# Graph transformer layer on one core: the front in seven parts, GpSimd making the centred rows of eight of 25 blocks

## The chip, the cores and the metric

One core of a Trainium2 chip runs the whole program. The metric is the device time of one execution in microseconds (us). Before the change it is 783.42 us, the median of three runs (782.71 to 783.50).

## What is computed

The input x has 6250 rows of 256 values. A layer norm gives `xn`. Three branches are added to x: a graph attention (four heads), a mixing branch of 1x1 convolutions in hyperbolic space, and, behind a second layer norm, a routed feed-forward layer. The change concerns only how the first two branches begin:

```python
xn = _layernorm(x, axis=-1)
# graph branch
xt = jnp.matmul(x, weight).reshape(-1, heads, out_ch)
alpha_l = jnp.einsum('ehd,hd->eh', xt[row], attn_l)
alpha_r = jnp.einsum('ehd,hd->eh', xt[col], attn_r)
# mixing branch
h = logmap0(proj(x, c), c)
h = conv1d(jnp.transpose(h, (1, 2, 0)), w_qkv, pad=2)   # one row long: a 256 x 768 product
```

`proj` clips the norm of a row and `logmap0` scales the row by arctanh(norm)/norm, so both branches need, for each row of x, its mean, its variance and a factor from the norm.

## The kernel before

The rows are cut into 25 blocks of 250 rows (125 partitions, two rows t to a partition). The program has one written-out order of instructions for each engine; engines meet at semaphores only. The **front** is all that stands before the first product with `w_qkv` (L1242). For a block b it does this:

- SyncE (SP) loads x in twelve loads (`LOADS`, L75, issued at L524): eight at the start, four later, each behind the store of a block named in `LOAD_AFTER` (L428).
- VectorE (DVE), `row_sums(b)` (L1627): two bn_stats. Then, for a **part** of several blocks at once (`PARTS`, L76: 2, 3, 4, 5, 6 and 5 blocks), the factors of its rows are worked out on tiny tiles (125 x 4 to 125 x 12): `row_square` (nine instructions, L1638 to L1652), two powers on GpSimd (POOL, L612 and L613), `row_clip` (three, L1658 to L1662), two logarithms on ScalarE (ACT, `row_logs`, L851 and L852), and `row_factors` (five, L1668 to L1676).
- DVE, `make_h(b)` (L1687): two tensor_scalar of 125 x 256, (x - mean) * factor, into a ring `hb` of four blocks (`HS`). It waits for the turn of block b-4.
- TensorE (PE), `turn_h(b)` (L1187): four transposes into PSUM bank b % 2. ACT, `keep_h(b)` (L893): one copy of 128 x 500 to SBUF.
- PE, `make_xt(b)` (L1199): four products of that copy with the graph weights, 125 x 264 each half. It waits for `keep_h(b)` and for `keep_xt(b - 2)`, which frees its bank. ACT, `keep_xt(b)` (L901): two copies with a scale. SP (L549) stores these rows to `xt_table` in HBM, from where GpSimd later gathers them (L623, L626).

The order around the change is written out by hand. PE turns block b and then makes the table rows of block b-1; ACT follows in the same order, with the parts' logarithms and the later weight loads (`later_load`, L861 to L887) between. `idle_work` (L1165) is a number of products whose result nobody reads; they stand where PE would otherwise wait. Before all this PE turns the graph weights (L1171) once they have landed (`wg_in`), ACT copies them (L847), PE multiplies them with the attention vectors (L1177) and ACT copies the result beside the weights (L857, `prep`), for which `make_xt(0)` waits. In the program before, `row_logs(0)` stands behind the copy of L847.

Behind the front PE runs the 75 steps of the QKV product (L1242), which start when the table rows of block 23 are kept, then the rest.

## Time and profile before

| | |
|---|---|
| median of three runs | 783.42 us (782.71 to 783.50) |
| profiled execution, device time | 782.98 us |
| its span, from the first to the last instruction | 780.8 us |
| PE busy | 746.4 us, 96% of the span |
| DVE, ACT, POOL busy | 587.1, 497.2, 510.4 us |
| first QKV product (L1242) | 74.25 us from the span's start |

Times in the trace are microseconds from the start of the span. The record of an instruction lasts until its result is written, and the next one on the same engine may start before that. So the spacing of starts tells what an instruction occupies, its end what a waiting engine sees. A PE product or transpose in f32 leaves one or two records: 36 records are 18 idle products, 8 are the four products of one `make_xt`, 4 the transposes of one `turn_h`.

### The profile page before, as it was taken

How to read it: one execution, taken by the hardware profiler on the slowest of the kernel's cores; microseconds unless marked ns; L12 is line 12 of the kernel's file. 1: busy time of each engine (PE TensorE's matmuls, PEld its weight loads, DVE VectorE, ACT ScalarE, POOL GpSimd, SP SyncE). 2: the span in 40 equal slices, each digit the busy share in tenths (PEclk: the TensorE clock that was granted, in tenths of full speed). 3: DMA queues.
4: the chain of work that ended last, by engine and by line, in shares of the span. 5: the costliest groups of instructions: out<-in, count | busy, mean ns of one | idle time of the engine just before them, and what ended most of it. 6: DMA issues, size and time to landing. Idle time of an engine off the chain costs nothing. (4 is left out here: it accounts for less than half of the span.)

```text
span 780.8 us, 17022 instructions
## 1 busy us (share of the span) xinstructions
PE 746.4 (96%) x5582; PEld 629.9 (81%) x5582; DVE 587.1 (75%) x1726; ACT 497.2 (64%) x1153; POOL 510.4 (65%) x693
## 2 busy tenths in 40 slices
PE   7999999999899999999929989999999999999996
PEld 7888888888666666666626678999999999999996
DVE  7973488788769988888897865666777667767676
ACT  2565335989899888888828616555555555555550
POOL 3340778777458888888826652676677766867654
PEclk9999999999999999999968999999999999999999
DMA  8665122222102211111110113000000000000001
GB/s 232 201 176 158 42 58 50 61 47 58 30 20 70 61 51 44 52 35 60 28 43 26 37 33 103 6 23 27 14 27 20 22 28 16 26 27 15 27 21 46
DMA packets 35546, 41.43 MB, mean 53 GB/s; under 512 B 11636, under 2 KB 20812, under 8 KB 35455
## 3 DMA queue, kind: packets, MB, share of 16 engines
q1 hardware_dynamic: 22471, 30.71, 13.1%
q0 software_dynamic: 8000, 6.82, 4.0%
q10 hardware_dynamic: 4984, 2.79, 1.5%
q8 instruction: 45, 0.74, 0.4%
q14 instruction: 46, 0.38, 0.2%
HBM read 25.59 MB, written 14.60 MB: 51 GB/s over the span
## 5 line engine op out<-in xcount | busy, mean ns | idle before, releaser
L1242 PE MATMUL ps<-Z,L 128*128 128x250 f32 x600 | 126.9, 373 | 0.0
L1242 PEld LDWEIGHTS ps<-Z,L 128*128 128x128 f32 x600 | 113.6, 189 | 13.2
L1097 ACT ACTIVATE Z<-Z,b1s 128x250 f32<-128x250 f32 x144 | 70.0, 503 | 70.5 <-DVE Z L2212 70.5
L1362 PE MATMUL ps<-wr,Z 128*125 128x256 f32 x400 | 92.7, 384 | 0.0
L942 ACT ACTIVATE Z<-Z,bn_o,bn_s 128x250 f32<-128x250 f32 x150 | 81.2, 599 | 1.0 <-DVE bn_o L1920 1.0
L1362 PEld LDWEIGHTS ps<-wr,Z 128*125 128x125 f32 x400 | 73.1, 188 | 10.2 <-issue 0.4
L1104 ACT ACTIVATE L<-ps 128x250 f32<-128x250 f32 x144 | 54.3, 379 | 42.1 <-PE ps L1492 40.1
L2212 DVE TENSOR_TENSOR Z<-ps,L 128x250 f32<-128x250 f32 x144 | 59.7, 416 | 18.3 <-PE ps L1492 15.9
L1252 PE MATMUL ps<-Z,pw 64*64 64x250 f32 x600 | 54.6, 386 | 15.6 <-issue 14.9
L1801 DVE BATCH_NORM_STATS2 L<-Z 128x6 f32<-128x250 f32 x140 | 49.3, 408 | 25.9 <-ACT Z L938 22.3
L623 POOL DMA_INDIRECT L<-xt_table,idst x36 | 44.2, 1228 | 34.8 <-issue 33.7
L938 ACT ACTIVATE Z<-ps 128x500 f32<-128x500 f32 x75 | 43.4, 579 | 30.9 <-PE ps L1242 24.5
L776 POOL TENSOR_TENSOR L<-Z 128x500 f32<-128x500 f32 x23 | 31.8, 1381 | 44.8 <-ACT Z L1097 44.8
L1492 PE MATMUL ps<-Z 128*128 128x250 f32 x192 | 56.4, 375 | 0.2 <-ACT Z L1097 0.2
L626 POOL DMA_INDIRECT asrc<-xt_table,isrc x40 | 48.4, 1210 | 12.2 <-issue 12.2
L1252 PEld LDWEIGHTS ps<-Z,pw 64*64 64x64 f32 x600 | 25.7, 133 | 36.5 <-issue 26.3
L1340 PE MATMUL ps<-L,ones 128*32 128x250 f32 x600 | 48.5, 384 | 2.0 <-ACT L L970 1.0
L1199 PE MATMUL ps<-L,Z 128*125 128x264 f32 x200 | 48.8, 388 | 0.8 <-ACT Z L893 0.5
L1531 PEld LDWEIGHTS ps<-Z 128*125 128x125 f32 x368 | 47.2, 187 | 2.0
L1531 PEld LDWEIGHTS ps<-L 128*125 128x125 f32 x368 | 47.1, 187 | 2.0
L1531 PE MATMUL ps<-Z 128*125 128x128 f32 x368 | 47.6, 272 | 0.0
L1531 PE MATMUL ps<-L 128*125 128x128 f32 x368 | 47.5, 272 | 0.0
(280 smaller groups left out, 2006.2 us busy)
## 6 DMA issues: line engine op xcount, KB each, us to landing
Z<-in_x SPq DMA_DIRECT2D x25, 250.0 KB
out<-L SPq DMA_DIRECT2D x24, 250.0 KB
xt_table<-L SPq DMA_DIRECT2D x25, 231.0 KB
Z<-in_x SPq DMA_DIRECT2D x4, 672.0 KB
Z<-in_x SPq DMA_DIRECT2D x5, 448.0 KB
g_table<-gg SPq DMA_DIRECT2D x25, 62.5 KB
gg<-g_table SPq DMA_DIRECT2D x25, 62.5 KB
Z<-in_w SPq DMA_DIRECT2D x2, 512.0 KB, 3.7
```

The lines of the kernel that those rows point to most:

```text
L942: a_.activation(zc(b, c), zc(b, c), ACT.Relu, bias=bn_o[:, c:c + 1], scale=bn_s[:, c:c + 1]).then_inc(done.sem, 1)
L1097: a_.activation(to, of, ACT.Gelu, bias=b1s[:, f // NF, f % NF:f % NF + 1]).then_inc(gelu_done, 1)
L1104: a_.activation(kp[:, s, k - 1], ps[:, bank, 0:BT], ACT.Copy).then_inc(product_kept[s].sem, 1)
L1199: last = mm(ps[0:TP, 2 + 2 * (b % 2) + t, 0:XT], h_raw(b, k)[:, t * TP:(t + 1) * TP], wg[:, k, :], start=(k == 0), stop=(k == KD - 1))
L1242: last = mm(ps[:, group_bank(n), h * BT:(h + 1) * BT], wq[:, k, c * 128:(c + 1) * 128], h_raw(b, k), start=(k == 0), stop=(k == KD - 1))
L1252: return mm(to[cols_], lhsT[rows_, HALF * a:HALF * a + HALF], rhs[rows_], start=True, stop=True)
L1340: last = mm(ps[32 * q:32 * q + 32, 5, 0:BT], ones[:, 0:32], of, start=(i == 0), stop=(i == 3), skip_group_check=True)
L1362: last = mm(res_bank(b, t), ob(b, c, 1)[:, t * TP:(t + 1) * TP], wr[:, c, :], start=(c == 0), stop=(c == NO - 1))
L1492: mm(ps[:, bank, 0:BT], of, by, start=first, stop=True, skip_group_check=True).then_inc(product[s].sem, 1)
L1531: last = mm(ps[0:TP, bank, 0:HD2], of[:, k], by[:, k], start=(first and k == 0), stop=(k == NF - 1), skip_group_check=True)
L1801: v_.bn_stats(to, ps[:, group_bank(n), h * BT:(h + 1) * BT] if last else zc(b, c)).then_inc(z_sums.sem, 1)
L2212: v_.tensor_tensor(to, ps[:, bank, 0:BT], kp[:, s, k - 1], ALU.add).then_inc(product_sum[s].sem, 1)
```

## The change

- `PARTS` has seven parts, of 1, 2, 3, 4, 5, 5 and 5 blocks.
- GpSimd makes the centred rows of blocks 0, 1, 2, 4, 6, 8, 11 and 12 (`POOL_H`) with the same tensor_scalar as DVE, written between the powers of the parts; DVE makes the other 17.
- PE turns block b and then makes the table rows of block b-2 in place of b-1, in the steady part; near the start some go in pairs. Idle products go from 18, 2, 3, 3 and 10 to 12, 2, 10, 2 and 4.
- ACT: `row_logs(0)` stands ahead of the copy of the turned graph weights, and all `row_logs` have new places.
- DVE has a new order of sums, parts and rows.
- The load of blocks 16 and 17 goes out behind the store of block 1 in place of block 0.

```diff
-    PARTS = ((0, 2), (2, 5), (5, 9), (9, 14), (14, 20), (20, NB))
+    PARTS = ((0, 1), (1, 3), (3, 6), (6, 10), (10, 15), (15, 20), (20, NB))
+    POOL_H = (0, 1, 2, 4, 6, 8, 11, 12)
...
-        FIRST_LOADS, LOAD_AFTER = 8, (0, 2, 3, 5)
+        FIRST_LOADS, LOAD_AFTER = 8, (1, 2, 3, 5)
...
-            for i, (b0, b1_) in enumerate(PARTS):
+            def row_powers(i):
+                b0, b1_ = PARTS[i]
                 js, w = slice(b0 * TB, b1_ * TB), (b1_ - b0) * TB
                 pool.wait_ge(row_dve, i * ROW_ALL + ROW_SQ)
                 g.tensor_tensor(rows[0:TP, 6, js], rows[0:TP, 5, js], phalf[0:TP, 0:w], ALU.pow).then_inc(row_pool, 1)
                 g.tensor_tensor(rows[0:TP, 7, js], rows[0:TP, 4, js], nhalf[0:TP, 0:w], ALU.pow).then_inc(row_pool, 1)
+
+            def pool_makes_h(b):
+                i = [i for i, (b0, b1_) in enumerate(PARTS) if b0 <= b < b1_][0]
+                pool.wait_ge(row_dve, (i + 1) * ROW_ALL)
+                if b >= HS:
+                    pool.wait_ge(h_turned.sem, h_turned.count(b - HS))
+                for t in range(TB):
+                    j = b * TB + t
+                    g.tensor_scalar(hb[0:TP, b % HS, t, :], x_raw(b)[:, t * D:(t + 1) * D], rows[0:TP, 0, j:j + 1],
+                                    rows[0:TP, 11, j:j + 1], ALU.subtract, ALU.mult).then_inc(h_pool.sem, 1)
+
+            row_powers(0)
+            pool_makes_h(0)
+            row_powers(1)
+            pool_makes_h(1)
+            pool_makes_h(2)
+            row_powers(2)
+            pool_makes_h(4)
+            row_powers(3)
+            pool_makes_h(6)
+            pool_makes_h(8)
+            row_powers(4)
+            pool_makes_h(11)
+            pool_makes_h(12)
+            row_powers(5)
+            row_powers(6)
...
-            for o in range(KD):
-                act.wait_ge(wg_turned, o + 1)
-                a_.activation(wgt[:, o], ps[:, 6 + o, 0:D], ACT.Copy).then_inc(wgt_made, 1)
             def row_logs(i):
                 js = slice(PARTS[i][0] * TB, PARTS[i][1] * TB)
                 act.wait_ge(row_dve, i * ROW_ALL + ROW_CLIP)
...
             row_logs(0)
+            for o in range(KD):
+                act.wait_ge(wg_turned, o + 1)
+                a_.activation(wgt[:, o], ps[:, 6 + o, 0:D], ACT.Copy).then_inc(wgt_made, 1)
             act.wait_ge(left_right, 1)
...
+            row_logs(1)
             keep_h(0)
             keep_xt(0)
-            row_logs(1)
             keep_h(1)
+            keep_h(2)
+            row_logs(2)
             keep_xt(1)
-            keep_h(2)
+            keep_xt(2)
             keep_h(3)
-            row_logs(2)
-            keep_xt(2)
+            keep_h(4)
             keep_xt(3)
-            keep_h(4)
             keep_h(5)
+            row_logs(3)
             keep_xt(4)
-            for b in range(6, NB):
+            keep_xt(5)
+            keep_h(6)
+            keep_h(7)
+            keep_xt(6)
+            row_logs(4)
+            keep_h(8)
+            keep_h(9)
+            keep_both(7)
+            keep_both(8)
+            keep_h(10)
+            keep_h(11)
+            keep_both(9)
+            for b in range(12, NB):
+                if b == 12:
+                    row_logs(5)
+                if b == 17:
+                    row_logs(6)
                 keep_h(b)
-                if b == 7:
-                    row_logs(3)
-                if b == 17:
-                    row_logs(5)
-                keep_both(b - 1)
-                if b == 11:
-                    row_logs(4)
+                keep_both(b - 2)
+            keep_both(NB - 2)
             keep_both(NB - 1)
...
-            idle_work(5, 18)
+            idle_work(5, 12)
...
-                pe.wait_ge(h_made.sem, h_made.count(b))
+                if b in POOL_H:
+                    pe.wait_ge(h_pool.sem, h_pool.count(POOL_H.index(b)))
+                else:
+                    pe.wait_ge(h_made.sem, h_made.count(b - len([c for c in POOL_H if c < b])))
...
             idle_work(7, 2)
             turn_h(0)
-            idle_work(7, 3)
+            idle_work(7, 10)
             make_xt(0)
+            idle_work(7, 2)
             turn_h(1)
-            idle_work(7, 3)
+            idle_work(7, 4)
+            turn_h(2)
             make_xt(1)
-            idle_work(7, 4)
-            pe.wait_ge(row_dve, ROW_ALL + ROW_CLIP + 2)
-            idle_work(7, 3)
-            pe.wait_ge(row_dve, 2 * ROW_ALL - 2)
-            idle_work(7, 3)
-            turn_h(2)
+            make_xt(2)
             turn_h(3)
-            make_xt(2)
+            turn_h(4)
             make_xt(3)
-            turn_h(4)
             turn_h(5)
             make_xt(4)
-            for b in range(6, NB):
+            make_xt(5)
+            turn_h(6)
+            turn_h(7)
+            make_xt(6)
+            turn_h(8)
+            turn_h(9)
+            make_xt(7)
+            make_xt(8)
+            turn_h(10)
+            turn_h(11)
+            make_xt(9)
+            for b in range(12, NB):
                 turn_h(b)
-                make_xt(b - 1)
+                make_xt(b - 2)
+            make_xt(NB - 2)
             make_xt(NB - 1)
             pe.wait_ge(wq_made, 6 * KD)
...
             def make_h(b):
-                for i, (b0, _) in enumerate(PARTS):
-                    if b == b0:
+                for i, (b0, b1_) in enumerate(PARTS):
+                    if b0 <= b < b1_:
...
             row_sums(0)
+            row_square(0)
             row_sums(1)
-            row_square(0)
-            row_sums(2)
             row_clip(0)
             row_factors(0)
+            row_sums(2)
+            row_square(1)
             row_sums(3)
...
```

The part of the DVE order that is left out has the same functions in another order, with seven parts in place of six and without `make_h` of the eight blocks.

**PE, from the start of the program.** First the order before: 

```order
L1165 MATMUL ps<-ident,ones 128x128 x18
L1171 MATMUL ps<-ident,L 128x128 x4
L1177 MATMUL ps<-attd,L 128x8 x4
L1165 MATMUL ps<-ident,ones 128x128 x2
L1187 MATMUL ps<-ident,L 128x125 x4
L1165 MATMUL ps<-ident,ones 128x128 x3
L1199 MATMUL ps<-L,Z 125x264 x4
L1187 MATMUL ps<-ident,L 128x125 x4
L1165 MATMUL ps<-ident,ones 128x128 x3
L1199 MATMUL ps<-L,Z 125x264 x4
L1165 MATMUL ps<-ident,ones 128x128 x10
L1187 MATMUL ps<-ident,L 128x125 x8
```

Then the order of the changed kernel (L1206 is the idle product, L1212 the turn of the weights, L1218 the attention product, L1231 the turn of a block, L1243 its table rows):

```order
L1206 MATMUL ps<-ident,ones 128x128 x12
L1212 MATMUL ps<-ident,L 128x128 x4
L1218 MATMUL ps<-attd,L 128x8 x4
L1206 MATMUL ps<-ident,ones 128x128 x2
L1231 MATMUL ps<-ident,L 128x125 x4
L1206 MATMUL ps<-ident,ones 128x128 x10
L1243 MATMUL ps<-L,Z 125x264 x4
L1206 MATMUL ps<-ident,ones 128x128 x2
L1231 MATMUL ps<-ident,L 128x125 x4
L1206 MATMUL ps<-ident,ones 128x128 x4
L1231 MATMUL ps<-ident,L 128x125 x4
L1243 MATMUL ps<-L,Z 125x264 x8
```

Before, two blocks are done and ten idle products stand behind them; now the idle products stand around blocks 0 and 1, and block 2 is turned before the table rows of block 1.

**POOL, behind its constants.** The rows of the changed kernel; L615 and L616 are the two powers of a part, L625 the new tensor_scalar of the centred rows. Before, only the powers of six parts stand here.

```order
L615 TENSOR_TENSOR L<-L,phalf 125x2
L616 TENSOR_TENSOR L<-L,nhalf 125x2
L625 TENSOR_SCALAR L<-Z,L 125x256 x2
L615 TENSOR_TENSOR L<-L,phalf 125x4
L616 TENSOR_TENSOR L<-L,nhalf 125x4
L625 TENSOR_SCALAR L<-Z,L 125x256 x4
L615 TENSOR_TENSOR L<-L,phalf 125x6
L616 TENSOR_TENSOR L<-L,nhalf 125x6
L625 TENSOR_SCALAR L<-Z,L 125x256 x2
L615 TENSOR_TENSOR L<-L,phalf 125x8
L616 TENSOR_TENSOR L<-L,nhalf 125x8
L625 TENSOR_SCALAR L<-Z,L 125x256 x4
```

The powers of the parts 1 to 4 are queued behind centred rows, and the other way round.

**ACT, behind its table load.** The rows of the changed kernel; L877 and L878 are the logarithms of a part, L883 the copy of the turned weights, L886 `prep`, L922 `keep_h`, L930 `keep_xt`.

```order
L877 ACTIVATE L<-L 125x2
L878 ACTIVATE L<-L 125x2
L883 ACTIVATE L<-ps 128x256 x2
L886 ACTIVATE L<-ps 128x8 x2
L877 ACTIVATE L<-L 125x4
L878 ACTIVATE L<-L 125x4
L922 ACTIVATE Z<-ps 128x500
L930 ACTIVATE L<-ps,L 125x264 x2
L922 ACTIVATE Z<-ps 128x500 x2
L877 ACTIVATE L<-L 125x6
L878 ACTIVATE L<-L 125x6
L930 ACTIVATE L<-ps,L 125x264 x4
```

Before, the logarithms of part 0 stood behind the weight copies, and those of part 1 behind `keep_xt(0)`; now both stand ahead of `keep_h(0)`, and those of part 2 behind `keep_h(2)`.

## Rows read from the trace of the kernel before

**Rows 1.** The page's busy times; share of the span and instructions behind each.

```profile
PE 746.4 (96%) x5582; PEld 629.9 (81%) x5582; DVE 587.1 (75%) x1726; ACT 497.2 (64%) x1153; POOL 510.4 (65%) x693
```

**Rows 2.** Busy time in one stretch: length, each engine (instructions), PEclk, DMA share, GB/s.

```profile
22.00:74.00 52.00, 51.36 (x277) 43.34 (x276) 37.84 (x173) 34.04 (x76) 13.80 (x7) 1.00 0.60 176
```

**Rows 3.** Timeline of PE: start, us, engine, line, what [idle before it, releaser].

```profile
2.35 6.87 PE L1165 MATMUL ps<-ident,ones 128*128 128x128 f32 x36 [2.35 <-POOL ident L606]
9.06 0.60 PE L1171 MATMUL ps<-ident,L 128*128 128x128 f32 x4
...
11.11 0.69 PE L1165 MATMUL ps<-ident,ones 128*128 128x128 f32 x4
13.19 0.65 PE L1187 MATMUL ps<-ident,L 125*128 125x125 f32 x4 [1.39 <-DVE L L1687]
...
19.75 2.39 PE L1165 MATMUL ps<-ident,ones 128*128 128x128 f32 x20
21.98 1.02 PE L1187 MATMUL ps<-ident,L 125*128 125x125 f32 x8
23.24 3.83 PE L1199 MATMUL ps<-L,Z 128*125 128x264 f32 x16 [0.25 <-ACT Z L893]
...
70.69 3.73 PE L1199 MATMUL ps<-L,Z 128*125 128x264 f32 x16
74.25 10.09 PE L1242 MATMUL ps<-Z,L 128*128 128x250 f32 x47
```

**Rows 4.** Idle products (L1165) in 6 to 7 and in 7.9 to 8.2 us: durations, first and last start.

```profile
L1165 PE MATMUL ps<-ident,ones x7: 421/421/421, 5.7 to 7.0; 128*128 128x128 f32 x7
L1165 PE MATMUL ps<-ident,ones x5: 274/275/368, 7.6 to 8.2; 128*128 128x128 f32 x5
```

**Rows 5.** Timeline of DVE, POOL and ACT in the first 18 us.

```profile
3.62 0.75 DVE L1627 BATCH_NORM_STATS2 L<-Z 125x6 f32<-125x256 f32 x2 [0.79 <-DMA Z<-in_x]
...
5.51 0.75 DVE L1627 BATCH_NORM_STATS2 L<-Z 125x6 f32<-125x256 f32 x2 [1.14 <-DMA Z<-in_x]
...
7.59 1.02 POOL L612 TENSOR_TENSOR L<-L,phalf 125x4 f32<-125x4 f32 x1 [5.29 <-DVE L L1652]
...
8.08 0.75 DVE L1627 BATCH_NORM_STATS2 L<-Z 125x6 f32<-125x256 f32 x2 [0.58 <-DMA Z<-in_x]
...
10.36 0.16 DVE L1668 TENSOR_TENSOR L<-L 125x4 f32<-125x4 f32 x1 [1.17 <-ACT L L852]
...
11.04 0.17 DVE L1676 RECIPROCAL L<-L 125x4 f32<-125x4 f32 x1
...
12.42 0.72 DVE L1687 TENSOR_SCALAR L<-Z,L 125x256 f32<-125x256 f32 x2
...
16.81 0.15 DVE L1658 TENSOR_SCALAR L<-L 125x6 f32<-125x6 f32 x1
...
17.14 0.20 ACT L852 ACTIVATE L<-L 125x6 f32<-125x6 f32 x1
```

**Rows 6.** POOL's instructions by line and form: count, busy us, mean ns, idle before.

```profile
L708 POOL TENSOR_TENSOR sg<-sg,nhalf 125x2 f32<-125x2 f32 x25 | 18.6, 743 | 2.1
...
L688 POOL TENSOR_SCALAR cc<-npw 125x2 f32<-125x2 f32 x25 | 7.7, 308 | 5.1 <-POOL npw L683 5.1
...
L612 POOL TENSOR_TENSOR L<-L,phalf 125x6 f32<-125x6 f32 x1 | 1.4, 1422 | 5.4 <-DVE L L1652 5.4
```

**Rows 7.** Timeline of DVE and POOL near the end: one form, alone and beside POOL.

```profile
643.25 0.48 DVE L2312 SCALAR_TENSOR_TENSOR pw<-L,zmv 125x256 f32<-125x256 f32 x1
...
644.79 1.60 POOL L765 TENSOR_TENSOR Z<-Z,L 125x256 f32<-125x256 f32 x2
...
644.91 0.90 DVE L2312 SCALAR_TENSOR_TENSOR wr<-brow,zmv,L 125x256 f32<-125x256 f32 x1
```

**Rows 8.** DMA issues up to 30 us: the graph weights; KB, us from issue to landing.

```profile
L<-in_w_gnn SPq DMA_DIRECT2D x1, 256.0 KB, 4.5
```

**Rows 9.** Timeline of POOL, the first gather behind the front.

```profile
78.81 1.47 POOL L623 DMA_INDIRECT L<-xt_table,idst  x1 [24.35 <-issue]
```

59 lines of the change are left out of this document (27 added, 32 removed).

## The prediction

> **What bounds the kernel now.** I read the page first: PE is busy 96% of the span and no other engine over 75% [rows 1]. So time is won only where PE stands idle or does work that nobody reads. Then the busy time by stretches, for the front: from 22 to 74 us PE is busy 51.36 of 52.00 us [rows 2], so its middle is PE's own work, with no other engine to blame. Then the timeline of PE alone [rows 3]. The reader is to see three things there. The idle products: 36 records (18 products) fill 2.35 to 9.06, 20 records (10 products) fill 19.75 to 21.98. The late first turn: PE stands idle for 1.39 us until 13.19, when DVE has made block 0. And the steady part: from the table rows of block 2 (23.24) to those of block 23 (70.69) lie 21 turns and 21 pairs of table rows, 47.45 us, 2.26 us a block, small waits included; the last two blocks of table rows take 74.25 - 70.69 = 3.56, so 1.78 each, which leaves 0.48 for a turn with its share of the waits. The first QKV product starts at 74.25.
>
> PE's work for 25 blocks is 25 x 2.26 = 56.5 us. Before 74.25, that would start at 17.7. It starts at 13.19 and then stands behind data: blocks 0 and 1 are done by 19.75, block 2 is not made, and DVE is the reason. The chain for block 0 shows it [rows 5]: sums at 3.62 and, because part 0 is two blocks, again at 5.51 when the second load lands; POOL's power at 7.59; the factors from 10.36, since the logarithms stand behind the copy of the weights on ACT; and the row itself only at 12.42, behind four more sums on DVE.
>
> **The change, part by part.**
>
> *The start of PE.* 12 idle products are 24 records. Seven starts lie between 5.7 and 7.0 [rows 4], 0.217 apart, so they end at 2.35 + 24 x 0.217 = 7.55. The graph weights have landed by then: their issue runs from 2.5 to 3.0 and takes 4.5 [rows 8], 7.0 to 7.5. From the turn of the weights to the idle products behind the attention products the trace has 11.11 - 9.06 = 2.05 [rows 3]; I add 0.2, because records last 421 ns until past 7 and 275 ns after (the page's granted clock says 1.00 all along; the durations show the lower level of 1.2 GHz and then 2.4) [rows 4]. So 9.8. Two idle products at 2.23/10 = 0.22 [rows 3]: 10.2. Here `turn_h(0)` can start. Then turn 0.45, ten idle products 2.23, table rows 1.78, two idle 0.45, turn 0.45, four idle 0.9: `turn_h(2)` at 16.4, if the rows are there. Behind that stand 23 turns, as before behind 21.98, and one block of table rows more: 16.4 + (74.25 - 21.98) + 1.78 = 70.45. That is **3.8 us earlier**. It keeps all the small waits of before, which a lag of two blocks may take away (another 0.3 to 0.6).
>
> *Are the rows there?* Block 0: sums end at 4.4; from the end of the sums to the power took 7.59 - 6.26 = 1.33; the power of two columns is 0.74 [rows 6]; POOL to DVE 0.15; clip to the end of the second logarithm 17.34 - 16.81 = 0.53; factors 11.21 - 10.36 = 0.85 [rows 5]. That is 8.0. Then POOL makes two rows.
>
> *The price of POOL's row.* The trace has no tensor_scalar of 125 x 256 on POOL. From below: 0.31 for one of two columns [rows 6]. From above: 0.80 for two inputs of 125 x 256 (1.60 for two) [rows 7]. I take the middle, 0.55, since it has the width of the second but one tensor to read. Block 0 is ready at 9.1, 1.1 before PE wants it. At 0.80 it still has half a microsecond.
>
> The page GPSIMD Engine Reference of the Trainium skill (section Engine selection) advises against elementwise work on this engine, roughly twice VectorE's time with two inputs and near line rate with one. Twice DVE's 0.36 would be 0.72, an estimate by that page, which moves the sum by some 0.3; rows here have no such instruction.
>
> *Blocks 1 and 2 (part 1).* The third load lands at 8.08 [rows 5]; sums to 8.8, square to 10.1, power 1.02, clip, logarithms and factors 1.5: 12.8. POOL has them at 13.9 and 15.0; PE wants them at 15.1 and 16.4. One thing is new here: `row_logs(1)` stands ahead of `keep_h(0)` on ACT, and `clip(1)` behind the sums of blocks 3 and 4. If their load lands by 10.4, ACT is free at 11.9 and the copy done at 12.5, before the table rows at 12.9. The trace shows no wait for that load, but asks for it only after 11.
>
> *The later parts.* From POOL's end of block 2 to block 4: power of six columns 1.42 [rows 6], then 0.15, 0.53, 0.85 and two rows 1.1, 4.1 in all; PE has two turns and two blocks of table rows in that time, 4.5. I walked the five queues in this way with such durations, each instruction waiting for its queue and its semaphores. The kernel before, walked so, starts the QKV product at 74.05 (traced 74.25). The changed one starts it at 69.9, with these reserves before PE wants a block: block 3 0.7, block 4 0.8, block 6 0.4, block 7 0.7, block 10 0.8, block 11 0.9, all others over 1.1 and from block 17 on over 3. So the two ways give 3.8 and 4.15; I take the first. DVE loses eight blocks of rows (8 x 0.65 = 5.2 us) and gains one part (2.5 us), neither on the path.
>
> *At no cost:* POOL's powers and rows are done by 50 us, long before its first gather at 78.81 [rows 9], which waits for the last table rows and moves with them. On the SP queue the load of blocks 16 and 17 goes one store later; DVE wants it past 29, its issue comes near 20. ACT's weight loads keep their distance to the end of the front within a turn, 0.45 us. DVE then still has batch-norm copies of 4.9 us that end about where its first QKV statistics begin: under 0.5, and not PE's.
>
> **Sum.** 782.98 - 3.8 = 779.2 for the profiled execution (span 780.8, 2.2 around it). Its time lies 0.44 under the median of 783.42; I put the forecast between, at **779.4**. What a measurement of this kernel can tell from no change is 0.2%, 1.6 us.
>
> **Rivals.**
>
> *A. The shared read port.* One DVE form with two inputs takes 0.48 beside a power on POOL's queue and 0.90 when it starts while POOL adds 125 x 256 [rows 7]. So such an instruction is held until POOL's wide one ends. The page SBUF — State Buffer of the Trainium skill (section Who interferes with whom) has this as an exclusive lock between a DVE instruction with two SBUF inputs and a GpSimd instruction that reads SBUF; the rows agree. Here `row_square` has six such instructions and `row_factors` three, and squares 2, 3 and 4 fall beside POOL's rows of blocks 1 and 2, 4, and 8. Each can lose at most what POOL has left there, 0.5 to 1.1 us. Up to 0.5 disappears in the reserves; at 0.8 the walk starts QKV 0.85 later, at 1.1 1.9 later. With POOL's row at 0.80 and no hold it is 0.85 later; with both 1.7. So 780.2 to 781.4. For it: the row of 0.90. Against it: the sums and DVE's own rows have one tensor input, and gaps between POOL's instructions let DVE in. Chance 0.20.
>
> *B. Slower: POOL's row at 1.2 us.* The place is the loop POOL row, power, clip, logarithm, factors, POOL row. At 1.2 block 4 comes 3.0 + 2.4 = 5.4 after block 2, against PE's 4.5; the walk has PE wait 1.2 before blocks 2, 1.5 before 3 and 4, 1.0 before 6, 1.8 before 10 and 11: QKV 1.4 later than before, 784.5. It decides at 1.1 us a row; at 0.9 the kernel is still over 2 us faster. Against it: half as much again as the dearest row of that width. Chance 0.04.
>
> *C. PE's clock.* Records drop to 275 ns after more than five microseconds of unbroken products [rows 4]. Now the unbroken stretch ends at 7.55, and narrow products and waits follow. If PE stays on its lower level through the ten idle products and block 0, these cost some 2.5 more: 781.9. Chance 0.05.
>
> *D. Given back behind the front.* QKV starts earlier but a later wait ends at the same time (a gather, batch-norm parameters). Nothing is tied to a fixed time that I can see. 782 to 784. Chance 0.08, with it that the load of blocks 3 and 4 lands past 11 or another unseen wait.
>
> *Forecast:* 0.63, its own range 778.3 to 780.2.
>
> **The numbers.** The range for 8 in 10 takes in the forecast, A and most of C: 778.3 to 781.9. Faster by over 0.2% (below 781.85): forecast, A and half of C, some of D, 0.85 less what I have not thought of: 0.82. Within 0.2%: 0.13. Slower: 0.05.
>
> **What would show it.** Right: first QKV product near 70.3; PE's first turn near 10.2; no wait of PE for `hb` above 0.2; POOL's row 0.4 to 0.65. Wrong: PE waiting for POOL's or DVE's rows at blocks 3, 4, 6, 10, 11 (A, B; DVE's tiny two-input instructions longer than 0.17 would tell A); records of 421 ns behind 8 us (C); QKV near 70 but the span shortened by less (D).

## The result, and the profile after

| | kernel before | changed kernel |
|---|---|---|
| time, median of 15 runs each | 782.38 us (780.72 to 783.50) | 784.31 us (783.57 to 785.99) |
| ratio, 95% interval | | 1.0026, 1.0019 to 1.0033 |
| profiled execution, span | 780.8 | 782.6 |
| first QKV product | 74.25 | 76.23 |

The change makes the kernel slower by 0.26%, where a gain of 3.8 us and a time of 779.4 had been forecast. Of the profiled executions' time 2.2 us lie outside the span before (782.98 - 780.8) and 1.8 after (784.48 - 782.6); what makes this difference no run shows. The page's busy times of the changed kernel answer to [rows 1]: PE has lost 2.4 us of products that nobody reads, POOL has gained 22.

```profile
PE 744.0 (95%) x5570; PEld 627.2 (80%) x5570; DVE 588.5 (75%) x1727; ACT 498.6 (64%) x1155; POOL 532.7 (68%) x711
```

The busy times of 22 to 74 us answer to [rows 2]: PE was busy 51.36 of 52 us there and is busy 48.27 now. POOL's time has doubled.

```profile
22.00:74.00 52.00, 48.27 (x257) 39.71 (x256) 36.01 (x169) 32.00 (x73) 27.48 (x18) 1.00 0.62 177
```

The timeline of PE answers to [rows 3] (start, us, engine, line, what, idle before and its releaser). L1206 are the idle products, L1231 the turns, L1243 the table rows, L1294 QKV.

```profile
6.89 0.66 PE L1212 MATMUL ps<-ident,L 128*128 128x128 f32 x4
...
10.28 0.65 PE L1231 MATMUL ps<-ident,L 125*128 125x125 f32 x4 [0.59 <-POOL L L625]
...
15.92 0.65 PE L1231 MATMUL ps<-ident,L 125*128 125x125 f32 x4 [0.46 <-POOL L L625]
...
18.33 0.65 PE L1231 MATMUL ps<-ident,L 125*128 125x125 f32 x4 [0.87 <-POOL L L625]
...
24.27 0.65 PE L1231 MATMUL ps<-ident,L 125*128 125x125 f32 x4 [1.16 <-POOL L L625]
...
31.67 1.07 PE L1231 MATMUL ps<-ident,L 125*128 125x125 f32 x8 [0.97 <-POOL L L625]
...
39.70 0.65 PE L1231 MATMUL ps<-ident,L 125*128 125x125 f32 x4 [0.25 <-DVE L L1739]
41.44 0.65 PE L1231 MATMUL ps<-ident,L 125*128 125x125 f32 x4 [1.09 <-POOL L L625]
...
76.23 3.96 PE L1294 MATMUL ps<-Z,L 128*128 128x250 f32 x18
```

PE's turns of blocks 0, 1, 2, 4, 6 and 11 wait for L625, POOL's rows: 0.59 + 0.46 + 0.87 + 1.16 + 0.97 + 1.09 = 5.14 us. The weights' turn comes at 6.89 (before at 9.06), so PE starts early enough, and everything won there is lost to POOL. The rows of blocks 8 and 12, the other two of the eight, keep PE waiting nowhere. POOL's timeline shows why the six do.

```profile
7.75 2.47 POOL L625 TENSOR_SCALAR L<-Z,L 125x256 f32<-125x256 f32 x2 [0.84 <-DVE L L1728]
...
13.43 4.84 POOL L625 TENSOR_SCALAR L<-Z,L 125x256 f32<-125x256 f32 x4 [0.67 <-DVE L L1728]
18.24 1.34 POOL L615 TENSOR_TENSOR L<-L,phalf 125x6 f32<-125x6 f32 x1
19.56 1.32 POOL L616 TENSOR_TENSOR L<-L,nhalf 125x6 f32<-125x6 f32 x1
21.59 2.64 POOL L625 TENSOR_SCALAR L<-Z,L 125x256 f32<-125x256 f32 x2 [0.71 <-DVE L L1728]
24.19 1.68 POOL L615 TENSOR_TENSOR L<-L,phalf 125x8 f32<-125x8 f32 x1
```

The instructions of the line itself (min/median/max in ns, first and last start):

```profile
L625 POOL TENSOR_SCALAR L<-Z,L x16: 1215/1232/1403, 7.8 to 42.6; 125x256 f32<-125x256 f32 x16
```

A row takes 1.23 us, where 0.55 was taken. The rows of blocks 1 and 2 fill POOL until 18.27; the power of part 2 can only start there, and VectorE's clip of that part stands still for it:

```profile
19.62 0.17 DVE L1710 TENSOR_SCALAR L<-L 125x6 f32<-125x6 f32 x1 [1.85 <-POOL L L615]
```

Then come clip, logarithms, factors and the row of block 4, ready at 24.23: 5.96 after block 2, against the 4.5 that PE needs for two turns and two blocks of table rows.

### The profile page after: what moved, and what is told of

Its sections match the earlier page's. It is cut to its first block and busy times, and to the rows that moved or that the text cites. A ratio compares the mean times of both kernels' runs of the same rounds, so it can differ in the third digit from the quotient of the medians.

```text
span 782.6 us, 17038 instructions
## 1 busy us (share of the span) xinstructions
PE 744.0 (95%) x5570; PEld 627.2 (80%) x5570; DVE 588.5 (75%) x1727; ACT 498.6 (64%) x1155; POOL 532.7 (68%) x711
## 5 line engine op out<-in xcount | busy, mean ns | idle before, releaser
L1294 PE MATMUL ps<-Z,L 128*128 128x250 f32 x600 | 126.9, 373 | 0.0
L1294 PEld LDWEIGHTS ps<-Z,L 128*128 128x128 f32 x600 | 113.6, 189 | 13.2
L1414 PEld LDWEIGHTS ps<-wr,Z 128*125 128x125 f32 x400 | 73.1, 188 | 10.2 <-issue 0.4
L1304 PE MATMUL ps<-Z,pw 64*64 64x250 f32 x600 | 54.6, 386 | 15.9 <-issue 15.5
L1243 PE MATMUL ps<-L,Z 128*125 128x264 f32 x200 | 48.0, 387 | 0.2 <-ACT Z L922 0.2
```

The lines of the kernel that those rows point to most:

```text
L1243: last = mm(ps[0:TP, 2 + 2 * (b % 2) + t, 0:XT], h_raw(b, k)[:, t * TP:(t + 1) * TP], wg[:, k, :], start=(k == 0), stop=(k == KD - 1))
L1294: last = mm(ps[:, group_bank(n), h * BT:(h + 1) * BT], wq[:, k, c * 128:(c + 1) * 128], h_raw(b, k), start=(k == 0), stop=(k == KD - 1))
L1304: return mm(to[cols_], lhsT[rows_, HALF * a:HALF * a + HALF], rhs[rows_], start=True, stop=True)
L1414: last = mm(res_bank(b, t), ob(b, c, 1)[:, t * TP:(t + 1) * TP], wr[:, c, :], start=(c == 0), stop=(c == NO - 1))
```

## The experiments

Durations, first QKV products and waits are of one profiled execution each, times are medians. "First QKV" is the first QKV product. The third column, a group of DVE's waits in the mixing stage, is told of under x6_qkv_later.

| run | first QKV | DVE's "issue" waits before the statistics: times, us | time | before, same chip | ratio, 95% |
|---|---|---|---|---|---|
| changed kernel | 76.2 | 2, 0.5 | 784.31 | 782.38 | 1.0026 [1.0019, 1.0033] |
| x1_rows_on_dve | 72.1 | 13, 4.8 | 782.64 | 782.36 | 1.0003 [0.9994, 1.0011] |
| x3_lag_two | 74.5 | 6, 1.6 | 782.35 | 782.36 | 0.9999 [0.9990, 1.0007] |
| x6_qkv_later | 74.1 | 13, 4.7 | 784.44 | 782.13 | 1.0021 [1.0011, 1.0032] |
| x7_act_rows | 72.4 | 4, 1.6 | 778.30 | 782.13 | 0.9946 [0.9932, 0.9961] |
| x8_pad_8 | 72.2 | 13, 4.7 | 782.62 | 782.42 | 1.0000 [0.9991, 1.0009] |
| x8_pad_16 | 72.0 | 12, 4.5 | 782.25 | 782.42 | 1.0000 [0.9990, 1.0009] |
| x8_pad_40 | 72.2 | 2, 0.5 | 779.58 | 782.42 | 0.9961 [0.9947, 0.9976] |
| x9_act_rows_2 | 70.0 | 4, 1.3 | 779.00 | 782.42 | 0.9954 [0.9940, 0.9969] |
| x10_act_rows_2_pad | 70.4 | 3, 1.0 | 778.52 | 782.30 | 0.9956 [0.9941, 0.9971] |
| x11_before_pad | 74.2 | 9, 3.5 | 783.10 | 782.30 | 1.0016 [1.0007, 1.0026] |
| x12_after_pad | 76.3 | 10, 4.1 | 786.32 | 782.30 | 1.0053 [1.0039, 1.0066] |

### All rows on VectorE (x1_rows_on_dve)

```diff
-    POOL_H = (0, 1, 2, 4, 6, 8, 11, 12)
+    POOL_H = ()
...
-            pool_makes_h(0)
...
             row_factors(0)
+            make_h(0)
```

and so on for the other seven, each in VectorE's order behind the factors of its part.

> The changed kernel with all 25 blocks' rows on DVE again (those of blocks 0, 1, 2, 4, 6, 8, 11, 12 put behind the factors of their part), everything else as changed. Theory P (the price of GpSimd's row, 1.23 us where 0.55 was taken, sits in the loop row, power, clip, logarithm, factor, and is the whole loss): the first QKV product moves from 76.2 to about 73.2 (walking the queues with the durations of rows gives 72.65, and the same walk of the changed kernel gives 75.65 where the trace has 76.23), the time is 3 us under the changed kernel's and about 1 us under that of the kernel before. Rival O (the orders, the lag of two blocks or the seventh part cost it themselves): QKV stays past 74.5 and the time at or over that of the kernel before. Rival D (DVE cannot carry the rows, which is why they were moved): PE waits for DVE's rows at blocks 3 to 12 by more than 3 us together, QKV past 75.

The first QKV product came at 72.1, 4.1 earlier than in the changed kernel and 2.1 earlier than before. PE's longest wait for a row is now

```profile
21.55 1.29 PE L1218 MATMUL ps<-ident,L 125*128 125x125 f32 x8 [0.70 <-DVE L L1726]
```

So POOL's rows cost the front 4.1 us, and seven parts with the new orders alone would gain 2.1. The expectation had been 73.2 and a time 1 us under the kernel before. But the time is that of the kernel before, within its interval. That the 2.1 us were not in it was the open question behind this run.

### What a row costs, by its form (x2_forms)

```diff
+                    if b in (0, 6):
+                        ins = g.tensor_scalar(to, of, factor, None, ALU.mult)
+                    elif b in (1, 8):
+                        ins = g.tensor_scalar(to, of, 0.01, 0.97, ALU.subtract, ALU.mult)
+                    elif b in (2, 11):
+                        ins = g.tensor_scalar(to, of, 0.97, None, ALU.mult)
+                    elif b == 12:
+                        ins = g.tensor_tensor(to, of, factor.broadcast_to([TP, D]), ALU.mult)
```

> The changed kernel; GpSimd's rows in other forms, so that the rows of these blocks are not the reference's: blocks 0 and 6 multiply by the factor alone (one operation, one column as scalar), 1 and 8 two operations with constants in place of the two columns, 2 and 11 one operation with a constant, 12 a tensor_tensor with the factor broadcast, 4 as it was. It measures the disputed price by itself. Theory two-operations: one operation costs about half (0.6 to 0.7 us), constants change nothing. Theory columns: constants cost about half, the number of operations changes nothing. Theory elements (the number of elements alone sets it): all forms cost 1.1 to 1.25. The two-input form of 125x256 took 0.73 to 0.80 elsewhere in this kernel, so the tensor_tensor should cost about that. In the time: where the forms fall to 0.6, the QKV product starts about 3 us earlier than in the changed kernel.

Its time (858.5 us) can't be compared, since other values in the blocks send later work down other paths; only POOL's rows are read. POOL's timeline:

```profile
7.78 1.86 POOL L628 TENSOR_SCALAR L<-Z,L 125x256 f32<-125x256 f32 x2 [0.84 <-DVE L L1739]
...
12.84 2.15 POOL L630 TENSOR_SCALAR L<-Z 125x256 f32<-125x256 f32 x2 [0.66 <-DVE L L1739]
14.95 1.67 POOL L632 TENSOR_SCALAR L<-Z 125x256 f32<-125x256 f32 x2
...
19.96 2.63 POOL L636 TENSOR_SCALAR L<-Z,L 125x256 f32<-125x256 f32 x2 [0.72 <-DVE L L1739]
...
37.81 1.22 POOL L634 TENSOR_TENSOR L<-Z,L 125x256 f32<-125x256 f32 x2
```

Per instruction of 125 x 256: tensor_scalar with one constant 0.84, with one column 0.93 (1.01 in block 6), with two constants 1.08, with two columns 1.31 (in block 4, as in the changed kernel, whose other rows take 1.21 to 1.30); tensor_tensor with the factor broadcast 0.61. Every form of tensor_scalar is dearer than either tensor_tensor, this one and the one of two whole tensors in [rows 7] (0.80), though it has one tensor less to read. That is what the bound from above in the prediction could not see. Of what had been expected, neither the number of operations nor the kind of scalar explains the price alone: a second operation adds 0.24 to 0.38, columns in place of constants 0.09 to 0.23. The tensor_tensor came out below its expected 0.73 to 0.80.

### The loop at half and at double the price (x4_row_at_061, x5_rows_twice)

```diff
-                    g.tensor_scalar(hb[0:TP, b % HS, t, :], x_raw(b)[:, t * D:(t + 1) * D], rows[0:TP, 0, j:j + 1],
-                                    rows[0:TP, 11, j:j + 1], ALU.subtract, ALU.mult).then_inc(h_pool.sem, 1)
+                    g.tensor_tensor(hb[0:TP, b % HS, t, :], x_raw(b)[:, t * D:(t + 1) * D],
+                                    rows[0:TP, 11, j:j + 1].broadcast_to([TP, D]), ALU.mult).then_inc(h_pool.sem, 1)
```

> The changed kernel with every row of GpSimd as a tensor_tensor times the factor alone (0.61 us each in an earlier run, against 1.23). The mean is not subtracted in eight blocks, so the values and the time of the whole differ; only the front is read. Theory (the loop of rows, powers, clip, logarithms and factors was right and only the price of a row was wrong): walking the queues with 0.61 a row starts the first QKV product at 69.6, and with the 0.2 to 0.6 by which the walk has been early, at 69.8 to 70.2; waits of PE before blocks 2, 4, 6, 10, 11 under 0.3 each. Rival (something else of the change holds the front: DVE's order, the logarithms on ACT): the first QKV product stays behind 73.

> The changed kernel with each of GpSimd's rows made twice, one after the other, so 2.4 us more a block; the result is that of the changed kernel. Theory (each row's time stands in the path of PE): the walk with 2.4 us a row starts the first QKV product at 94.7, 18.5 later than the changed kernel's 76.2, the waits of PE being about 3.5 before blocks 2, 4, 6 and 11; time about 803. Rival (the rows are beside the path and the loss has another cause): under 5 us more.

x5_rows_twice issues each row once more ahead of itself, and was run once. Its first QKV product came at 95.9, 19.7 later than the changed kernel's, and its time was 805.2. The queues walked with 2.4 us a row had said 94.7. So at this price all eight added pairs stand in PE's path, each of 2.43 to 2.47 us. (PE's granted clock was low in parts of this front, 0.52 from 14 to 16 us behind a wait of 3.13; this is in the 19.7.)

x4_row_at_061 leaves out the subtraction of the mean in these blocks, so that its time (826.8, one run) can't be compared. Its first QKV product came at 72.2: four microseconds earlier than the changed kernel, PE's waits for POOL gone, but 2.0 to 2.4 later than expected. PE's timeline shows what took their place: a wait for the graph weights, one for ScalarE's copy of block 0, and two for rows of VectorE:

```profile
7.32 0.66 PE L1212 MATMUL ps<-ident,L 128*128 128x128 f32 x4 [0.64 <-DMA L<-in_w_gnn]
...
13.18 2.05 PE L1243 MATMUL ps<-L,Z 128*125 128x264 f32 x8 [0.41 <-ACT Z L922]
...
21.93 1.07 PE L1231 MATMUL ps<-ident,L 125*128 125x125 f32 x8 [0.95 <-DVE L L1739]
...
37.22 1.07 PE L1231 MATMUL ps<-ident,L 125*128 125x125 f32 x8 [0.36 <-DVE L L1739]
```

The timelines of DVE and POOL in that run show why VectorE was late:

```profile
13.62 2.35 POOL L625 TENSOR_TENSOR L<-Z,L 125x256 f32<-125x256 f32 x4 [1.02 <-DVE L L1728]
14.21 0.61 DVE L1690 TENSOR_TENSOR L<-L 125x6 f32<-125x6 f32 x1
14.75 0.16 DVE L1691 TENSOR_TENSOR L<-L 125x6 f32<-125x6 f32 x1
14.83 0.58 DVE L1692 TENSOR_TENSOR L<-L 125x6 f32<-125x6 f32 x1
...
15.44 0.55 DVE L1696 TENSOR_SCALAR L<-L 125x6 f32<-125x6 f32 x1
...
20.45 1.42 DVE L1739 TENSOR_SCALAR L<-Z,L 125x256 f32<-125x256 f32 x2
20.49 1.23 POOL L625 TENSOR_TENSOR L<-Z,L 125x256 f32<-125x256 f32 x2 [1.12 <-DVE L L1728]
```

Three instructions of `row_square(2)` take 0.55 to 0.61 instead of 0.16, and the two rows of block 3 take 1.42 instead of the 0.74 that the pair of block 5 takes in the same run: 1.3 + 0.7 = 2.0 us that VectorE is held while POOL works on 125 x 256. That is rival A. Of the hold 0.95 + 0.36 = 1.3 us reach PE, and the rest of the delay is the other two waits. In the changed kernel, with POOL's rows as tensor_scalar, it is nearly absent: beside such a row L1692 and L1700 of `row_square(1)` take 0.38 and L1696 and L1698 of `row_square(2)` 0.32 and 0.24, the others their usual 0.16. So a cheaper row, made with tensor_tensor, brings in the mechanism of A where that of B was, at a gain of 2.0 in the first QKV product, not of 3.8. What a tensor_scalar at 0.61 would do no run shows.

The Trainium skill, SBUF — State Buffer, section Who interferes with whom, has a pair of ports that one of the two engines holds for a whole instruction, which touches VectorE's instructions with two SBUF inputs, or in a fast two-port mode. The 0.61 and 0.58 of two tensor_tensor agree, though the one between them took 0.16; that POOL's tensor_scalar, which reads SBUF too, held so little is not what that rule would make one expect.

### A lag of two blocks alone (x3_lag_two)

```diff
             for b in range(7, NB):
                 turn_h(b)
-                make_xt(b - 1)
+                make_xt(b - 2)
```

in PE's loop and likewise `keep_both` in ACT's, on the kernel before.

> The kernel before with the lag of two blocks alone, from block 7 on, on PE and ACT; six parts, all rows on DVE. Theory P: the steady part of PE was already its own work, so nothing changes but one small wait, the QKV product starts at 74.0 to 74.3 and the time is the same within 0.3 us. Rival O: it starts later by 0.5 or more.

782.35 against 782.36, first QKV product 74.5. The lag gives nothing where the rows are in time, and costs nothing.

### Is an earlier QKV worth anything? (x6_qkv_later)

```diff
             make_xt(NB - 1)
+            idle_work(7, 10)
```

on x1_rows_on_dve.

> The kernel with seven parts and all rows on VectorE (first QKV product at 72.1, time equal to before within 0.1%), and ten products that nobody reads between the last table rows and the first QKV product, 2.2 us of PE. If a later or earlier start of QKV is passed on to the end, 782.6 + 2.2 = 784.8. Rival (what the front gains is taken up by a wait behind it): 782.6, no change, which would also explain why 2.1 us at the first QKV product were not in the time.

QKV at 74.1, 2.0 later, and 784.44, 1.8 us more than x1_rows_on_dve: what comes late there is late at the end. So rival D, a later wait with a fixed end, is out, and x1_rows_on_dve must lose its 2.1 us on its own account.

PE's timeline shows where. In each kernel PE has one wait of some 14 us near 400 us; first the kernel before, then x1_rows_on_dve:

```profile
407.78 0.65 PE L1252 MATMUL ps<-Z,pw 64*64 64x250 f32 x1 [14.13 <-issue]
```

```profile
407.94 0.65 PE L1291 MATMUL ps<-Z,pw 64*64 64x250 f32 x1 [14.17 <-issue]
```

From the first QKV product to the start of that wait PE takes 393.65 - 74.25 = 319.4 us before and 393.77 - 72.14 = 321.6 in x1_rows_on_dve (319.6 in the changed kernel): the 2.1 us that were won are lost on this way. The waits of DVE between 195 and 475 us differ most in one row (what waited, for what: us in total, times, longest); "issue" is a wait for nothing that the profile shows. First the kernel before, then x1_rows_on_dve, then the changed kernel, and the line is in each the statistics of x1 in the mixing stage:

```profile
DVE st L2062 <- issue: 1.4, 4, 0.4
```

```profile
DVE st L2104 <- issue: 4.8, 13, 0.8
```

```profile
DVE st L2109 <- issue: 0.5, 2, 0.3
```

PE's timeline of x1_rows_on_dve has three waits that the kernel before has not:

```profile
245.27 0.60 PE L1389 MATMUL ps<-sel,L 128*125 128x2 f32 x4 [0.85 <-ACT L L1066]
...
258.60 0.39 PE L1291 MATMUL ps<-Z,pw 64*64 64x250 f32 x1 [0.25 <-issue]
...
322.01 0.39 PE L1291 MATMUL ps<-Z,pw 64*64 64x250 f32 x1 [0.70 <-issue]
```

Together 1.8 us. x6_qkv_later has the same three, at the same instructions, some 1.8 us later in time: 0.85, 0.23 and 0.64. So they go with the program and not with the moment. One thing in which the programs differ is the number of VectorE instructions ahead of the mixing stage, and the next runs change that alone. (It is not all: x3_lag_two has the VectorE instructions of the kernel before, and 6 of these waits for 4, the two more of 0.26 and 0.17 us. So a difference of two in the third column says nothing.)

### The same kernel, shifted in VectorE's stream (x8_pad_8, x8_pad_16, x8_pad_40)

```diff
             make_h(24)
+            for i in range(40):
+                v_.memset(unread[:, i:i + 1], 0.0)
```

> The kernel with seven parts and all rows on VectorE (first QKV product at 72.1, 2.1 before the kernel before, and yet the same time), with eight memsets of one column, that nobody reads, behind VectorE's last row (0.06 us each). That kernel and the one with QKV 2.2 later both show 13 waits of VectorE of 0.2 to 0.8 us for nothing that the profile shows before the same statistics of the mixing stage (4.8 us in all), the kernel before only 4 (1.4), and waits of PE of 0.85, 0.25 and 0.70 that the kernel before has not. Theory (these waits hang on where an instruction stands in VectorE's stream, not on time): shifting the stream by eight moves them; another number of such waits than 13, the first QKV product unmoved at 72.1, and with few of them 780.5 to 781. Rival (they hang on the data, or on what the seven parts changed): the same 13 waits and 782.6.

> The same with sixteen memsets, which brings VectorE's number of instructions in the front 32 above that of the changed kernel (1727 in all, 2 such waits) and 16 above the one with all rows on VectorE (1743, 13 waits). Theory: again another pattern of waits than with none or eight; first QKV product 72.1; time between 780.5 and 782.6 by their number. Rival: the same 13 waits and 782.6.

> The same with forty memsets, some 3 us of VectorE behind its last row. Theory: another pattern of waits; first QKV product 72.1; time between 780.5 and 782.6 by their number. Rival 1: the same 13 waits and 782.6. Rival 2 (VectorE's work behind its last row is on the path): the time grows with the number of memsets, by up to 3 us.

Eight and sixteen did nothing that can be measured: 13 and 12 waits, 782.6 and 782.3. That speaks against the theory as it was put, that any shift gives another pattern. Forty instructions that nobody reads made the kernel 3.1 us faster than none (779.58 against 782.64, ratio to before 0.9961 against 1.0003), with the first QKV product unmoved at 72.2. Of the 13 waits of VectorE before these statistics two are left, as in the changed kernel; of PE's three the first is down to 0.19 and the others are gone. PE's way from the first QKV product to its wait of 14 us is 319.6 us again, where it is 321.5 and 321.9 with eight and sixteen. VectorE's longest waits for "issue" that are left in 195 to 475 us:

```profile
DVE L L1993 <- issue: 1.3, 1, 1.3
...
DVE se L2086 <- issue: 0.6, 2, 0.3
DVE st L2107 <- issue: 0.5, 2, 0.2
```

This run has the front of x1_rows_on_dve and as few waits as the changed kernel, so it is the one to hold against the changed kernel: 4.0 us earlier at the first QKV product and 4.7 less in time (779.58 against 784.31, each on its own chip). That is the price of POOL's rows with the pattern of the waits taken out. What in the forty memsets changes the pattern is not shown: they shift the instructions behind them, and they also take VectorE's time, though only 0.9 us (59.0 to 59.9) and not the 3 us that had been expected.

### Is the measured loss such an accident? (x11_before_pad, x12_after_pad)

The same forty memsets behind `make_h(24)` of the kernel before and of the changed kernel.

> The kernel before with the same forty memsets. Theory: first QKV product unmoved at 74.3; 4 waits (1.4 us) of VectorE before the statistics change their number; the time moves by -1 to +2. Rival (the memsets help by themselves): 779.6, 2.8 less.

> The changed kernel with the same forty memsets. It has 2 such waits (0.5 us) and none of PE that hangs on them, so it had a good pattern already. Theory: QKV at 76.2, time 784 to 786.5, not faster; the loss of 2 us is the front's and no accident of the position. Rival (the loss of the changed kernel is such an accident): 782.4 or less.

No: the changed kernel had a good position already. Shifted, it shows 10 waits where it had 2, and PE waits of 0.29, 0.50 and 0.59 where it had one of 0.19:

```profile
DVE st L2112 <- issue: 4.1, 10, 0.8
```

786.32 us, 2.0 more than without. (Part of that lies ahead of these statistics: PE waits 1.34 us at 207 us for batch-norm parameters, where it waited 0.56, and VectorE shows two groups of "issue" waits at L1851, 1.8 us in all, that the changed kernel has not.) The kernel before goes from 4 waits to 9 and from 782.3 to 783.1. So forty memsets as such don't help; they change a pattern, for better in one kernel and for worse in two. PE's way to its wait of 14 us goes along each time: 321.9 for 319.6 in the changed kernel, 320.3 for 319.4 in the kernel before. Between the two kernels in question the pattern differs by 0.9 us of VectorE's waits, in favour of the changed one, and PE's way from the first QKV product to the last product of the mixing stage is nearly the same, 376.5 and 376.7 us. The 1.9 us by which the changed kernel is slower are the front's 2.0.

### Versions that beat both (x7_act_rows, x9_act_rows_2, x10_act_rows_2_pad)

ScalarE can make a row in one activation if it gets -mean x factor as a column, which costs VectorE one instruction a part:

```diff
+                v_.scalar_tensor_tensor(out=r[7], in0=r[0], scalar=-1.0, in1=r[11], op0=ALU.mult, op1=ALU.mult).then_inc(row_dve, 1)
...
+                    a_.activation(hb[0:TP, b % HS, t, :], x_raw(b)[:, t * D:(t + 1) * D], ACT.Identity,
+                                  bias=rows[0:TP, 7, j:j + 1], scale=rows[0:TP, 11, j:j + 1]).then_inc(h_act.sem, 1)
```

> Rows of blocks 0 to 4, 6 to 8 and 11 on ScalarE instead of GpSimd (one activation with scale and bias each, 0.36 us taken from its other ones of this width), with one more operation of VectorE a part for the bias, all orders drawn up anew for that. The walk starts the first QKV product at 69.0, so 69.2 to 69.8 in the trace, 5 us before the kernel before; if that is passed on to the end, 777.5; if only as much as in the run with all rows on VectorE, 779.5. Rival (ScalarE, with its copies for PE behind the rows, becomes the bound): first QKV product at 73 or later, time 782 or more.

The first version gave 778.30, but its first QKV product came at 72.4, not at 69.2 to 69.8. Two prices were wrong again: four rows take ScalarE 2.07 us (0.5 each, not 0.36), and VectorE waits 0.53 for the load of blocks 5 and 6 at 13.05 ahead of the factors of part 1. ScalarE's timeline, and what it does to PE:

```profile
14.98 2.07 ACT L923 ACTIVATE L<-Z,L 125x256 f32<-125x256 f32 x4 [2.41 <-DVE L L1792]
```

```profile
16.12 0.79 PE L1271 MATMUL ps<-ident,L 125*128 125x125 f32 x4 [2.03 <-ACT L L923]
...
17.99 4.67 PE L1283 MATMUL ps<-L,Z 128*125 128x264 f32 x16
```

Behind that wait of 2.03 us PE's granted clock is low, 0.62 from 16 to 18 us and 0.53 from 18 to 20, and the table rows of two blocks take 4.67 instead of 3.73: some 0.9 us more.

> The second version with rows on ScalarE (blocks 0, 1, 2, 4, 7, 9, 11), its orders drawn up with what the first one showed: a pair of rows takes ScalarE 1.0 us and not 0.72, the fourth and fifth load land at 10.7 and 13.0, so the sums of block 5 stand behind the factors of part 1, the wait of PE of 2.0 before block 1 falls to 0.6 or less. The walk starts the first QKV product at 70.4, where it gave 71.7 for the first version (traced 72.4): so 70.4 to 71.2, 1.2 to 2 us earlier than the first version, which took 778.3; forecast 776.5 to 777.5. Rival (the front's start is worth less than the pattern of VectorE's waits in the mixing stage): 778 to 780.

The second version, with both prices set right, starts QKV at 70.0, 0.4 us before the earliest forecast, but its time is 779.0, no better than the first, where 776.5 to 777.5 had been forecast; the rival's 778 to 780 came true. The profiled executions show part of this: from the last product of the mixing stage to the end of the span the second version takes 331.4 us (445.5 to 776.9), the first 329.9 (449.4 to 779.3), for a reason that no run shows. What the first owes its 778.3 to stays open too: by its first QKV product it should take some 780.4, and its profiled run did take 781.06, the longest of five (the others 777.85 to 779.76).

> The second version with rows on ScalarE (first QKV product at 70.0, 779.0) and forty memsets that nobody reads behind VectorE's last row, as in the run where they took the 13 waits before the statistics of the mixing stage away. Theory (the pattern hangs on the position in VectorE's stream): QKV stays at 70.0; the version has 4 such waits (1.3 us) and one wait of PE of 0.45, so at most 1 us is to be had: 778.0 to 779.0 if they go, up to 781 if the shift brings more. Rival (the memsets help by themselves, whatever the pattern): 776.2, 2.8 less, as there.

With forty memsets 778.52, 3 waits instead of 4: no change that can be told, as the position theory has it, and not the 2.8 us of the rival. All three versions are 3.4 to 3.8 us under the kernel before, and 5.3 to 6.0 under the changed one, each on its own chip.

## Why the prediction was wrong

**The price of POOL's row** is the step that failed. 0.55 was taken as the middle of 0.31 and 0.80; measured 1.23. The end from above was no end: it was a row of the same width but of another instruction, and tensor_scalar is the dearer one on this engine at every form that x2_forms tried. The sentence that it "has the width of the second but one tensor to read" reasoned from the number of inputs, and the trace had nothing that bore this out. The estimate of 0.72 beside it doubled VectorE's time, and was too low as well.

**Rival B** had mechanism, place and nearly the size: 1.2 us a row, PE waiting 1.2 before block 2 (measured 0.46 + 0.87 before 1 and 2), 1.5 before 3 and 4 (1.16), 1.0 before 6 (0.97), 1.8 before 10 and 11 (0.25 + 1.09), time 784.5 (784.31). QKV came 2.0 later and not 1.4; the loop took 5.96 and not 5.4, since clip, logarithms and factors took 2.0 and not 1.5 (19.58 to 21.59), with sums between them on VectorE, and the two rows 2.64 and not 2.4. Its chance of 0.04 rested on the false bound alone. The forecast had named the point from which it decides, 1.1 us a row; what was missing was a chance worthy of an operation that no row showed.

**The start of PE** was right, and 0.7 early: the weights' turn at 6.89 and the first turn possible at 9.5 (x1_rows_on_dve starts it at 9.47), where 7.55 and 10.2 had been forecast. The idle products ran at 275 ns, the level of 2.4 GHz, from 6.1 us on, where those of the kernel before were at 421 until 7.4 [rows 4]. This moment differs between executions: in x8_pad_40 and x9_act_rows_2 the records are of 421 ns until past 8 us, and the first turn starts at 10.6 and 10.5. The forecast's 10.2 lies between.

**Rival C** (PE on its lower level) did not happen in the changed kernel, whose granted clock is 1.00 throughout the front. It did in other runs: beside the late rise in those two, the clock fell behind the 2.03 us wait in x7_act_rows, and, in x3_lag_two and x11_before_pad, behind the wait of 1.39 us that the kernel before has too and that left the clock at 1.00 there (granted clock 0.50 from 14 to 16 us, with records of 421 ns again). None of it moved the first QKV product of x3_lag_two or x11_before_pad by more than 0.3 us against the kernel before, or that of x8_pad_40 by more than 0.1 against x1_rows_on_dve.

**Are the rows there?** Block 0 was ready at 10.22 and not at 9.1, blocks 1 and 2 at 15.9 and 18.3 and not at 13.9 and 15.0, nearly all by the price of the row: POOL took up block 0 at 7.75 and block 1 at 13.43, 0.3 before and 0.6 behind the sum's 8.0 and 12.8. **The later parts**: 4.1 forecast for the loop, 5.96 measured, of which 1.5 is the two rows' dearer price (2.64 for 1.1).

**The size of the gain with the right price** was off as well. With a row at 0.61 the forecast's 3.8 us were 2.0 (x4_row_at_061). Of the 1.8 that are missing 1.3 are PE's waits for rows of VectorE, which rival A held; A had been given at most 0.5 to 1.1 an instruction and up to 1.9 in all, and the instructions measured 0.4 each. A further 0.4 is a term that the sum had put at nothing: with `row_logs(1)` ahead of `keep_h(0)` on ScalarE, the copy of block 0 was done at 13.1 and not at 12.5, and PE waits 0.41 for it (0.74 in x1_rows_on_dve); in the changed kernel POOL's late row of block 0 hides this. With all rows on VectorE the gain was 2.1. So at nearly its own price, and with a tensor_tensor, the forecast would have missed by nearly 2 us.

**At no cost** held: the first gather moved with the front (81.32 against 78.81), the last table rows with it, and from the first QKV product to the end of the span the two kernels take the same time (706.6 us before, 706.4 after). **The lag of two** took no waits away, as the forecast had cautiously left out.

**Rival D** was wrong as a mechanism, but the observation it asked for, QKV earlier and the span not, did occur in x1_rows_on_dve: 2.2 us were lost between the first QKV product and PE's wait near 400 us, with 13 waits of VectorE in place of 4. That forty idle instructions take away both the waits and the loss is shown; why VectorE waits there is not.

## What to carry to other kernels

A bound for an instruction that the trace does not show must come from a row of the same operation, or it is no bound: same width and fewer inputs was wrong by half as much again here. When an operation is put on an engine that a loop goes through (here POOL, whose power each part needs), its price counts on the path at every turn, so the question to ask first is at what price the loop becomes longer than the work it hides behind, and the chance should follow from how far the knowledge of the price reaches, not from the middle of it. When a forecast says that a wait of PE disappears, ask what the next one is: here the copy on ScalarE and VectorE's rows took back nearly half of the gain. And forty instructions that do nothing moved the time by 3 us of 780 in work that they never touch: before a small gain or loss is put down to the edit, shift the stream in that way and look again.

## What the runs showed of the hardware

- GpSimd's tensor_scalar on 125 x 256 takes 0.84 to 1.31 us by its form, its tensor_tensor 0.61 with a broadcast input; VectorE makes the same row in 0.37. The Trainium skill, GPSIMD Engine Reference, section Engine selection, calls GpSimd with one input roughly as fast as line rate and with two about half as fast as VectorE; here the instruction with one input was the slower one, at 3.3 times VectorE's.
- A tensor_tensor of GpSimd holds some small VectorE instructions (0.55 to 0.61 for 0.16) and VectorE's own rows (1.42 for a pair of 0.74); a tensor_scalar of GpSimd on the same tiles holds the small ones by some 0.2 at most (0.38 and 0.40 for 0.16) and a pair of rows by the same (0.90).
- PE's granted clock in the same front differs between executions: the idle products reach 275 ns at 6.1 us in the changed kernel and past 8 in x8_pad_40, and a wait of 1.39 us left the clock at 1.00 in the kernel before and not in x3_lag_two and x11_before_pad.
- VectorE's waits for nothing that the profile shows, before one pair of instructions in a stage of 25 like blocks, number 2, 3, 4, 6, 9, 10, 12 or 13 in these kernels. Where forty idle instructions are all that differs, 13 and 2 waits go with times 3.1 us apart, 2 and 10 with 2.0 (784.31 and 786.32), 4 and 9 with 0.8 (782.3 and 783.1). PE's way from the first QKV product to its wait near 400 us is 319.3 to 319.8 us with 2 to 6 of them (320.1 in x7_act_rows), 320.3 with 9, and 321.4 to 321.9 with 10 to 13. The Trainium skill, Runtime: NRT & Kernel Launch, section Instruction fetch mechanics, has each engine's instructions streamed in from memory in blocks of 256, a crossing mostly hidden. Whether these waits are such crossings no run here shows. The 13 of x1_rows_on_dve lie within some 860 recorded instructions of VectorE, where blocks of that size would have three or four crossings (an estimate by that page), so most of them would need another cause; shifts of 8 and 16 left the pattern nearly alone and one of 40 did not.
